# Batch 0: one engine per pair of output tiles, and the transposes of Bx of batch 1 in mid-slot

## What is computed

```python
def _L0_cond_ref(x, A, B, adapter_ids):
    Bx = jnp.einsum('bni,bri->bnr', x, B[adapter_ids])
    return jnp.einsum('bnr,bor->bno', Bx, A[adapter_ids])
def _L1_cond_ref(x, language_ids, W, Wr, A, B):
    base = jnp.einsum('btd,od->bto', x, W)
    logits = jnp.einsum('btd,ed->bte', x, Wr) + bias
    topw, topi = jax.lax.top_k(logits, 2)
    ...
    h = jnp.einsum('btd,erd->bter', x, A)
    return base + 2.0 * jnp.einsum('bter,bte,eor->bto', h, gates, B)
x = x + _L0_cond_ref(x, ...)
x = x + _L1_cond_ref(x, ...)
```

## Time and profile before

| | us |
|---|---|
| median of 3 runs (lowest, highest) | 1573.11 (1572.71, 1574.83) |
| the profiled execution, its own time | 1572.13 |
| its span, first to last instruction | 1570.3 |
| TensorE busy, share of the span | 1545.7, 98% |
| VectorE busy | 1224.2, 78% |
| ScalarE busy | 713.9, 45% |
| mean granted TensorE clock | 0.997 |

### The profile page before, as it was taken

One profiled execution on the slowest core, in us unless ns is written; L12 is line 12 of the kernel. 1 busy time (PEld: TensorE's weight loads), 2 busy tenths in 40 slices (PEclk: granted clock), 3 DMA queues, 4 the chain that ended last, 5 costly groups with the idle time before them and its releaser, 6 DMA issues.

```text
span 1570.3 us, 20339 instructions
## 1 busy us (share of the span) xinstructions
PE 1545.7 (98%) x7430; PEld 1298.9 (83%) x7430; DVE 1224.2 (78%) x1630; ACT 713.9 (45%) x911; POOL 138.1 (9%) x181
## 2 busy tenths in 40 slices
PE   9889999999999999999999999999999999999998
PEld 9768878888888888888888888888888888888887
DVE  6987768877699777897688876987769976787665
ACT  6422222545445444454444544454444544445443
POOL 1565545000000000000000000000000000000000
PEclk9999999999999999999999999999999999999999
DMA  8899999697867777777676876769776777666564
GB/s 217 242 249 288 265 228 253 211 250 199 228 215 209 225 200 231 229 216 207 213 229 203 243 217 208 220 201 240 209 221 216 213 229 196 204 225 213 203 215 160
DMA packets 303110, 347.05 MB, mean 221 GB/s; under 512 B 204890, under 2 KB 236682, under 8 KB 302346
## 3 DMA queue, kind: packets, MB, share of 16 engines
q1 hardware_dynamic: 293602, 314.28, 69.7%
q0 software_dynamic: 9136, 30.94, 6.0%
q10 hardware_dynamic: 272, 0.52, 0.1%
HBM read 278.52 MB, written 66.72 MB: 220 GB/s over the span
## 4 chain that ended last, share of the span: by engine, by line
PE 88%; SPq 4%; DVE 3%; DMA 2%; issue 1%; ACT 1%; POOL 0%; DVEq 0%; POOLq 0%; ACTq 0%
PE pb L820 26%; PE pb L821 26%; PE pb L822 26%; PE pb L378 4%; PE pb L380 3%; SPq L292 2%; SPq L669 2%; PE pb L533 2%; DMA raw<-in_L_cond_W_dram 1%; DVE raw L684 1%; DMA ost<-in_L_cond_B_dram 1%; DVE xl L558 1%; DVE wl L816 1%; PE pb L319 0%; ACT wh L812 0%
## 5 line engine op out<-in xcount | busy, mean ns | idle before, releaser
L812 ACT CAST wh<-raw 128x1024 fp32r<-128x1024 f32 (+1 forms) x453 | 475.4, 1049 | 715.4 <-PE pb L822 687.1
L816 DVE TENSOR_TENSOR wl<-raw,wh 128x1024 fp32r<-128x1024 f32 (+1 forms) x453 | 556.9, 1229 | 273.8 <-ACT wh L812 272.7
L820 PE MATMUL pb<-wh,sh 128*128 128x512 f32 x1568 | 612.9, 391 | 0.5 <-DVE ost L870 0.5
L821 PE MATMUL pb<-wl,sh 128*128 128x512 f32 x1568 | 611.6, 390 | 0.0
L822 PE MATMUL pb<-wh,sl 128*128 128x512 f32 x1568 | 611.2, 390 | 0.0
L822 PEld LDWEIGHTS pb<-wh,sl 128*128 128x128 f32 x1568 | 294.3, 188 | 62.8
L820 PEld LDWEIGHTS pb<-wh,sh 128*128 128x128 f32 x1568 | 294.5, 188 | 56.2 <-DVE wl L816 0.9
L821 PEld LDWEIGHTS pb<-wl,sh 128*128 128x128 f32 x1568 | 294.6, 188 | 55.1
L378 PE MATMUL pb<-awb,xah 128*128 128x304 f32 x512 | 138.6, 304 | 0.7 <-DVE xal L355 0.7
L380 PE MATMUL pb<-awb,xal 128*128 128x256 f32 x512 | 134.3, 279 | 0.0
L820 PE MATMUL pb<-wh,xh 128*128 128x512 f32 x256 | 102.6, 401 | 5.2 <-DVE xl L558 3.5
(11 more groups left out here) (155 smaller groups left out, 1300.1 us busy)
## 6 DMA issues: line engine op xcount, KB each, us to landing
raw<-t_scr SPq DMA_DIRECT2D x392, 512.0 KB, 3.9
xst<-in_x_dram SPq DMA_DIRECT2D x448, 64.0 KB, 3.9
out_dram<-ost SPq DMA_DIRECT2D x72, 256.0 KB, 3.8
raw<-in_L_cond_W_dram SPq DMA_DIRECT2D x124, 128.0 KB, 4.9
raw<-bt_scr SPq DMA_DIRECT2D x28, 512.0 KB, 3.6
out_dram<-u SPq DMA_DIRECT2D x56, 256.0 KB, 2.8
t_scr<-raw POOLq DMA_DIRECT2D x32, 256.0 KB, 4.6
t_scr<-tst POOLq DMA_DIRECT2D x16, 512.0 KB, 6.1
```

Of the source, the lines that this page charges most:

```text
L812: e.copy(pair_split(wh, g), pair_source(g)).then_inc(c_wh, 1)
L816: e.tensor_tensor(out=pair_split(wl, g), in0=pair_source(g), in1=pair_split(wh, g).bitcast(f32), op=ALU.subtract).then_inc(c_wl, 1)
L820: e.matmul(o, h, wh[:, g % RING, k, :], start=start, stop=False)
L821: e.matmul(o, h, wl[:, g % RING, k, :], start=False, stop=False)
```

## The change

Two things in batch 0, each only in the order or the engine of work that stays the same.

1. Chunks 0 to 2: tiles t = 0 and 1 are both copied by ScalarE (at slots 8, 17, 26), tiles t = 2 and 3 both by VectorE (at slots 10, 19, 28). `wait_first` waits on the semaphores accordingly. Chunk 3 stays as it was.
2. `bx_transpose(1)` moves, in TensorE's list, from ahead of slot 27's first half (`first_products(27, 0)`) to behind it, ahead of the second half.

```diff
--- before.py
+++ after.py
@@ -826,8 +826,12 @@
         def first_bank(c, t):
             return (0, 1, 2, 3, 6, 7)[(4 * c + t) % 6]
 
+
         def wait_first(e, c, t):
-            e.wait_ge((c_evd, c_eva)[t % 2], 2 * c + 1 + t // 2)
+            if c == 3:
+                e.wait_ge((c_evd, c_eva)[t % 2], 7 + t // 2)
+            else:
+                e.wait_ge((c_eva, c_evd)[t // 2], 2 * c + t % 2 + 1)
 
         def first_products(e, i, h):
             c, k = divmod(i, 9)
@@ -864,7 +868,7 @@
                 e.wait_ge(d_ts[1], sums_in(1, SLOTS0))
             elif c or t >= 2:
                 e.wait_ge(d_ost[0], 32 * (2 * c + t // 2))
-            if t % 2:
+            if (t % 2 if c == 3 else t < 2):
                 e.copy(ost[:, first_place(c, t), :], pb[:, first_bank(c, t), :]).then_inc(c_eva, 1)
             else:
                 e.tensor_copy(ost[:, first_place(c, t), :], pb[:, first_bank(c, t), :]).then_inc(c_evd, 1)
@@ -1427,8 +1431,6 @@
                     hg_transpose(e, 0)
                 if i in (1, 2):
                     bt_transpose(e, 2 * i - 2)
-                if i == 27:
-                    bx_transpose(e, 1)
                 if i == 28:
                     aux_adapted(e, 1)
                 if i == 29:
@@ -1440,6 +1442,8 @@
                     first_gated(e, i)
                 else:
                     first_products(e, i, 0)
+                if i == 27:
+                    bx_transpose(e, 1)
                 if i in (1, 2):
                     bt_transpose(e, 2 * i - 1)
                 for u in DELTAS0.get(i, ()):
@@ -1501,8 +1505,9 @@
                         sum_hi(e, 1, 0, kp)
                 if i in (17, 25):
                     aux_low(e, 1, (i - 17) // 8)
-                if i in EVACUATED:
-                    first_evacuate(e, EVACUATED[i][0], EVACUATED[i][1] + 1)
+                if i in EVACUATED and EVACUATED[i][1] == 0:
+                    for t in range(2):
+                        first_evacuate(e, EVACUATED[i][0], t)
                 if i == 35:
                     for t in (1, 3):
                         first_evacuate(e, 3, t)
@@ -1587,8 +1592,9 @@
                         sum_lo(e, 1, 0, kp)
                 if i in (17, 25):
                     aux_sum(e, 1, (i - 17) // 8)
-                if i in EVACUATED:
-                    first_evacuate(e, EVACUATED[i][0], EVACUATED[i][1])
+                if i in EVACUATED and EVACUATED[i][1] == 2:
+                    for t in range(2, 4):
+                        first_evacuate(e, EVACUATED[i][0], t)
                 if i == 35:
                     for t in (0, 2):
                         first_evacuate(e, 3, t)
```

## The result

The changed kernel took 1578.33 us in the median of 12 executions (1572.01 to 1581.37); the kernel before, on the same chip, 1573.34. The ratio is 1.0021 (95%: 1.0011 to 1.0030), that is 1.7 to 4.7 us more. The forecast was 1574.3 us with a range up to 1576.1: right in sign and in the mechanism at slot 29, too small in size. In all, the changed kernel was measured in four sessions (ratios 1.0021, 1.0014, 1.0024, 1.0009): 46 executions with a median of 1576.7, beside 165 of the kernel before with 1573.8 (a slow one of 1707.75 is left out), so +2.9 us. The first session was the most unfavourable by its medians, 5.0 us apart; in the other three they lie 2.1, 3.8 and 1.6 us apart, with 1576.18, 1577.44 and 1575.55 us for the changed kernel. That the first came out as high as 1578.33 is in part chance.

The account below looks back on a forecast made before the run. TensorE, busy 98% of the span, was taken as the bound, leaving only its stalls. Copies 0, slot 27 -3.7, new wait +3.3, clock +1.6: together +1.2 us on 1573.11, so 1574.3 us, range 1570.9 to 1576.1.

Parts of the forecast that it names:

- the clock's +1.6 us behind slot 29: Behind slot 29's new stall the granted clock falls to about 0.5 for some 3 us, costing 1.6 us.
- part 1's 0: Regrouping the copies in chunks 0 to 2 gains zero, since SP's queue and the DMAs set when blocks of W arrive.
- The copies' own stalls: TensorE's waits for VectorE's copies, 0.63 us in chunk 0 and 1.11 us in chunk 1, go.
- slower than before: Rival: a grown stall near 209.35 also drops the clock, +2.8 us in all, 1575.9 us; chance 0.11.
- Its point between 1.54 and 2.08 us: The stall length from which the clock falls behind a TensorE stall was taken to lie between these values.
- Slot 27, -3.7 us: Moving the transposes removes slot 27's stall of 2.08 us and its slow-clock tail of 1.6 us.
- The new wait, 3.3 us, L533 0.4 us earlier than before: At slot 29 TensorE stalls 3.3 us for VectorE's copy; L533 starts 0.4 us earlier, estimated between 0.1 and 0.6.
- The range: The whole kernel's time was to lie from 1570.9 to 1576.1 us, about 0.11 left below and 0.06 above.

Follow-up runs that it names:

- e1: The changed kernel with only the copies regrouped, the transposes staying ahead of slot 27; +0.9 thousandths against the kernel before.
- e5: The kernel before, unchanged, measured again for a second profile; its trace has the longest span of all, 1579.0 us.
- e4: The changed kernel again, unaltered, for a second profile; ratio 1.0014 to the kernel before.
- e3: The changed kernel with VectorE's copy of chunk 2's t = 2 ahead of slot 28's block sums; by medians 2.1 us below e4.
- e6: The changed kernel with delta(1, 0) moved behind the first half of slot 29; ratio .9993 to the kernel before.
- e10: The changed kernel again, unaltered, for a third profile; ratio 1.0024 to the kernel before.
- e8: The changed kernel with delta(1, 0) in mid-slot 29 and the router and expert products of slots 10 and 23 at their slot's end; ratio .9975.
- e12: e8 with the copies grouped as they were before the change; ratio .9978 to the kernel before.
- e11: The kernel before, unchanged, for a third profile; the two repeat measurements of that kernel against itself gave 1.0008 and 1.0001.

## Why the prediction failed, by its own steps

Two terms of the sum failed: the clock's +1.6 us behind slot 29, which measured 2.4 in the mean, and part 1's 0, which was a loss of about 0.7 us. The rest of the distance to 1578.33 is, as far as the later sessions show, the chance of the first.

**The copies' own stalls**: right. The 0.63 and 1.11 us are gone in all traces of the changed kernel, and part 1 alone brings no gain (e1).

**Part 1 is zero, its bounds zero and 1.11 us gained**: wrong, and with no bound on the side of a loss. The step was that the arrival of the blocks of W, set by SP's queue and the DMAs, does not move when the copies do. At slot 10 it moved, later: SP's issue of those loads took 8.0 to 9.2 us in every trace with the new copies, 7.0 to 7.8 with the old, and from slot 8 to slot 17 the changed kernel takes 0.7 us more. That fits e1, 0.9 thousandths (1.4 us) above the kernel before. The stalls for xal at slots 10 and 23 were read as 0.23 and 0.47 us from one trace; in the other six traces of the two kernels they lie between nothing and 3.6 us, and some are followed by a fall. For slot 23 it is not settled whether the copies cause any of it: in e5 the unchanged kernel had the worst of these stalls. The rival "slower than before", a fall behind slot 23, happened in e4, one of four traces of the changed kernel, and in e5, one of three of the kernel before. Its point between 1.54 and 2.08 us, from which a stall decides, is not there: stalls of 1.78 us (e3) and 1.84 (e6) were followed by a fall, two of 3.2 us (e10) were not.

**Slot 27, -3.7 us**: the stall went in full, as forecast. The kernel before did not always pay the 1.6 us of tail, and where it didn't, slot 29 took most of it back (e5). As the forecast lets slot 29 decide the end, this error cancels.

**The new wait, 3.3 us, L533 0.4 us earlier than before**: right. It was 3.3 to 3.7 us in four traces, with the landing of slot 28's store as its cause. Where no fall lies behind slot 23, L533 came 35.0 to 35.2 us behind that slot, before 35.4 to 35.5, so 0.3 us earlier: between the two ends of the estimate, near the 0.4 taken. By the earlier trace rows VectorE needs 2.18 us from L725 to the end of the first copy; now it is about 2.6 (240.07 to 242.66): L725 kept its 0.43 us, L729 took 0.83 beside GpSimd's L738 of 0.96 (0.74 before). The Trainium skill's "SBUF — State Buffer", section "SBUF: two separate sides", has the two exclude each other, and lets the one that starts first go through. The rows agree: L725 started 0.05 us ahead of L738 and ran at its usual length, L738 and VectorE's next, L729, took longer.

**The clock behind slot 29, +1.6 us**: the mechanism was right, the size was not, and this is the larger of the two terms that failed. One low stretch of the usual length was assumed. All four traces of the changed kernel have the fall, two with 3.4 us at half rate and two with 6.8. From L533 to the end they took 1328.2 us in the mean (1327.4 to 1328.9), the kernel before 1325.8 (1325.5 to 1326.1): 2.4 us instead of 1.6, and up to 3.4. With the 0.3 us gained ahead of it that is +2.1 us, and with the 0.7 us of slots 8 to 17 +2.8, beside the +2.9 us of the pooled medians; that they agree so closely is luck, with three and four traces that differ by more. In the forecast the tails of slots 27 and 29 cancel (-1.6, +1.6). The mean granted clock of all executions says otherwise: 0.9948 against 0.9957, 0.0009 x 1575 = 1.4 us more lost to the clock, give or take about 1 us.

**The range**: it took the spread of one mechanism, and left out that executions of the changed kernel differ more than its two terms do. Its upper end of 1576.1 us lies between the medians of the later sessions (1575.55, 1576.18, 1577.44). The traced execution of the kernel before was the luckiest of its three (slot 23 at 209.4, then 215.5 and 211.8).

Not tried: the copy of t = 2 in e3's place together with an earlier store, which would take away slot 33's wait as well.

## What to carry to other kernels

When a stall is moved, price its tail again in the new place, with the chance that the clock falls and with twice its usual length as the upper end. Look in several traces of the kernel before, not one, at where TensorE waits when it comes early: the place that pins it is there already, and a gain ahead of it is not a gain. Two small waits can be cheaper than their sum in one piece, and the cheapest cure for either is to put work that waits for nothing ahead of the row that waits (e6, e8, e12).

## What the runs showed of the hardware

The same stall is followed by a fall of the clock to 1.2 GHz in one execution and not in the next. A stall of 2.08 us in front of the same row was followed by 0.50 (e11) and by 1.00 (e5); two of 3.2 us by 1.00 (e10), one of 1.78 us in e3 by 3.4 us of half rate. All seven of 3.28 us and more were followed by a fall, and none of the twelve of 1.1 to 1.6 us. The low stretch came in two lengths, 3.4 and 6.8 us, and cost about half of either. The store of slot 28's sums took 7.8 us from GpSimd's issue to its landing with and without the change (7.5 to 7.9 in the other traces of the two kernels), though TensorE finished slot 28 3.9 us earlier against slot 23 (31.5 us behind its first row, before 35.4): this time did not hang on TensorE.
